# One scale chain in the quantised feed-forward, an fp32 value product in two attentions, and another routing order in mixer 3

## What is computed

```python
def _quantize_activations_groupwise(x):      # 5 groups along the batch
    ...
        gamma = jnp.max(jnp.abs(ag))
        xq = ... jnp.clip(ag * QB / (gamma + EPS), -QB + EPS, QB - EPS)
def _bitlinear(x, W, b):
    Wb = _binarize_weights_groupwise(W)
    y = jnp.einsum('btc,oc->bto', x, Wb) + b
    return _quantize_activations_groupwise(y)
h = _bitlinear(x, W1, b1)
h = jax.nn.gelu(h, approximate=False)
out = _bitlinear(h, W2, b2)

x = x + _L0_conv_ref(_ln_c(x), ...)   # then the feed-forward above, and so on
```

## Time and profile before

| | before |
|---|---|
| median of 3 runs | 862.85 us (858.54, 862.85, 864.74) |
| the profiled execution | 860.89 us |
| span of its trace | 859.1 us, so 1.8 us lie outside it |
| mean granted PE clock | 0.935 of full speed |
| busy share of the span | PE 91%, DVE 69%, POOL 65%, ACT 50% |

### The profile page before, as it was taken

How to read it: one execution, slowest core, us unless ns; L and a number is a source line. 1 busy time by engine, 2 the same in 40 slices (tenths; PEclk the granted TensorE clock), 3 DMA queues, 4 the chain that set the end, 5 groups by cost and what they waited for, 6 DMA issues and landing times.

```text
span 859.1 us, 27761 instructions
## 1 busy us (share of the span) xinstructions
PE 779.6 (91%) x10760; PEld 641.8 (75%) x10760; DVE 589.5 (69%) x1609; ACT 428.5 (50%) x777; POOL 556.4 (65%) x885
## 2 busy tenths in 40 slices
PE   4897678699899999969997999999799999999996
PEld 3776566588688888958876688888777776888886
DVE  6677477678577777848874477787776773776754
ACT  3564563366544444457773553535445555444441
POOL 5645523455287887867773687788565674788764
PEclk9696698799999999989998999999967999999999
DMA  6611100000311101000011011010000011110030
GB/s 165 125 12 30 35 1 2 2 3 3 78 54 36 50 28 29 3 1 2 0 46 30 28 31 30 27 56 3 2 1 2 0 29 29 33 55 27 28 84 20
DMA packets 39145, 26.17 MB, mean 30 GB/s; under 512 B 27132, under 2 KB 31981, under 8 KB 39045
## 3 DMA queue, kind: packets, MB, share of 16 engines
q1 hardware_dynamic: 38302, 24.41, 11.2%
q10 hardware_dynamic: 742, 0.38, 0.2%
HBM read 7.87 MB, written 1.57 MB: 11 GB/s over the span
## 4 chain that ended last, share of the span: by engine, by line
PE 81%; DVE 10%; ACT 3%; issue 3%; POOL 2%; POOLq 0%; ACTq 0%; DVEq 0%
PE PS L1679 22%; PE PS L1652 9%; PE PS L1653 8%; PE PS L1656 4%; PE PS L1401 3%; PE PS L1767 3%; PE PS L1754 3%; PE PS L1387 3%; PE PS L1778 2%; PE PS L1787 2%; PE PS L1388 2%; PE PS L1797 2%; PE PS L1568 2%; PE PS L1480 2%; PE PS L1847 1%
## 5 line engine op out<-in xcount | busy, mean ns | idle before, releaser
L712 ACT ACTIVATE H<-PS,B 128x512 f32<-128x512 f32 x288 | 173.7, 690 | 194.7 <-PE PS L1656 194.7
L1679 PEld LDWEIGHTS PS<-M,H 128*64 128x64 f32 x4608 | 192.3, 137 | 21.7 <-issue 17.5
L1679 PE MATMUL PS<-M,H 128*64 128x96 f32 x4608 | 205.1, 248 | 1.8 <-DVE X L1196 1.8
L1196 DVE SCALAR_TENSOR_TENSOR X<-PS,G,X 128x96 f32<-128x96 f32 (+1 forms) x384 | 121.7, 318 | 96.6 <-PE PS L1679 86.3
L480 POOL TENSOR_TENSOR msum<-stats 128x4 f32<-128x4 f32 (+1 forms) x61 | 16.1, 263 | 137.7 <-DVE stats L895 111.3
L1652 PE MATMUL PS<-XH,M1h 128*128 128x512 f32 x192 | 78.7, 410 | 0.0
L490 POOL TENSOR_TENSOR XN<-X,mean 128x384 f32<-128x384 f32 x56 | 47.0, 840 | 48.9 <-PE PS L1401 48.9
L1653 PE MATMUL PS<-FHL,M1l 128*128 128x512 f32 x192 | 77.3, 402 | 0.0
L516 POOL TENSOR_TENSOR PF<-G,B 128x1536 f32<-128x1536 f32 x24 | 66.2, 2759 | 10.2 <-DVE G L1187 10.2
L524 POOL TENSOR_TENSOR ex<-euler,dl 128x16 f32<-128x16 f32 x24 | 69.9, 2912 | 1.7 <-DVE dl L1160 1.6
L494 POOL TENSOR_TENSOR rs<-ve,half 128x4 f32<-128x4 f32 (+1 forms) x61 | 65.4, 1072 | 4.8
(11 more groups left out here) (245 smaller groups left out, 1818.3 us busy)
## 6 DMA issues: line engine op xcount, KB each, us to landing
FHL<-XH SPq DMA_DIRECT2D x36, 192.0 KB, 2.5
FHL<-XL SPq DMA_DIRECT2D x36, 64.0 KB, 2.1
X<-XH SPq DMA_DIRECT2D x12, 192.0 KB, 2.5
raw<-L_ffn_w SPq DMA_DIRECT2D x3, 576.0 KB, 5.1
M<-L_ffn_w SPq DMA_DIRECT2D x3, 576.0 KB, 5.0
XH<-XL SPq DMA_DIRECT2D x24, 64.0 KB, 1.9
out<-X SPq DMA_DIRECT2D x8, 192.0 KB, 2.6
X<-x SPq DMA_DIRECT2D x3, 384.0 KB, 6.7
```

What stands on the lines that cost most here:

```text
L712: act.activation(H[p][:, c, :], bank(UB[c]), ACT.Gelu, bias=B1[e][:, c:c + 1]).then_inc(gelu_a, 1)
L1196: ins = dve.scalar_tensor_tensor(xt(g, t), bank(4 + t % 2)[:, e * C:(e + 1) * C], G[:, t, e:e + 1], xt(g, t), ALU.mult, ALU.add)
L1679: ins = pe.matmul(Y[rows, x * C:(x + 1) * C], H[p][:, j, t * P + rows.start:t * P + rows.stop], M2[e][:, j, :], start=c == 0, stop=c == CH ...
```

## The change

It has three parts.

1. **Feed-forward.** The two chains of scales become one (`maxima`, `scale_rows`, `spread`, `scales`): the transpose takes two columns, the first maximum of group q and the second of group q-2. The product with `gdg` spreads both numbers. `Y2` has two buffers. The bias products of `down` are gone; POOL adds the bias to the copied result (`ffn_bias`), and for the last group DVE adds it on the way out of PSUM. On ACT `ffn_out(q-1)` stands behind the GELU of group q (before: ahead of it). `ffn_stats(2)` stands ahead of the last `X` sum of attention 0. The second absolute maxima of the last two groups share their stretch with the softmax of group 8, the first of attention 1, whose scores are now made ahead of the last `down` products.
2. **Attentions.** ACT makes a whole copy `XV` of each transposed group (`whole`), and V is one fp32 product by 8 pieces (`values`) in the place of 12 products in three terms. Its weights `WV` are fetched by three more transfers; two more rows of ones are set at the start. In attention 0 the products of k and q of group g+2 stand ahead of P times V of group g, and so do their copies on ACT.
3. **Mixer 3.** On ACT `routing_relu` stands ahead of the first `mix_image`; on DVE `routing_out` and `routing_star` stand ahead of `mix_x`.

The core of the diff:

```diff
+        def chain(q):
+
+            return sum(2 + 2 * (2 <= x < FG) for x in range(q))
+
...
-            for q in range(FG):
+            def ffn_rows(q):
                 normalise(q, EPS_T, FT, fst_v, fag_p, X[:, q * FT * C:(q + 1) * FT * C], FX, ft_pe, fxn_p)
+
+            def ffn_bias(r):
+                pool.wait_ge(y2_a, r + 1)
+                pool.tensor_tensor(Y2[r % 2], Y2[r % 2], b2bc[:].unsqueeze(1).to_broadcast([P, FT, C]), ALU.add).then_inc(y2_p, 1)
+
+            for q in range(4):
+                ffn_rows(q)
+            ffn_bias(0)
+            ffn_rows(4)
+            ffn_bias(1)
             prep(2, 1, 0)
+            ffn_bias(2)
+            ffn_bias(3)
             prep(2, 1, 1)
...
+            def whole(m, p):
+                after(act, xt_used, m - 1)
+                act.activation(XV[p][0:C, :], turned(m), ACT.Copy).then_inc(xv_a, 1)
...
+                    def copy_keys():
+                        after(act, s_pe, n + 2)
+                        if ka == 1:
+                            act.wait_ge(q_pe, n + 3)
+                            act.activation(qT[0:C, :], bank(QB01[1], 512, C), ACT.Copy, scale=QSCALE).then_inc(q_a, 1)
+                        act.wait_ge(k_pe, n + 3)
+                        if ka == 1:
+                            act.activation(KT[0:C, :], bank(KB[1], 512, C), ACT.Copy).then_inc(k_a, 1)
+                        else:
+                            for h in range(HEADS):
+                                rows = slice(h * DH, (h + 1) * DH)
+                                ins = act.activation(kT[rows, h, :], PS[rows, KB[0], :], ACT.Copy)
+                            ins.then_inc(k_a, 1)
+                            act.wait_ge(q_pe, n + 3)
+                            act.activation(qT[0:C, :], bank(QB01[0], 512, C), ACT.Copy, scale=QSCALE).then_inc(q_a, 1)
+
+                    if ka == 0 and has(g, 2):
+                        copy_keys()
...
                 if q == FG - 1:
                     prep_hi(8, 0)
-                if q > 0:
+                    whole(8, 0)
                     ffn_out(q - 1)
                 for c in range(CH):
                     act.wait_ge(cl_v, 3 * q + c + 1)
                     after(act, fd_pe, 2 * (q - 1))
                     act.activation(YH[q % 2][:, c, :], Y1[q % 2][:, c, :], ACT.Gelu, scale=qs[:, 0:1]).then_inc(ge_a, 1)
+                if 0 < q < FG - 1:
+                    ffn_out(q - 1)
...
-                if has(g, 1):
-                    mix_image(g, p, 0)
                 if has(g, 2, 2):
                     routing_relu(g + 2)
                 if has(g, 1):
+                    mix_image(g, p, 0)
                     mix_image(g, p, 1)
...
+            def scale_rows(q):
+                n = columns(q).stop - columns(q).start
+                dve.wait_ge(g_pe, 2 * q + 1)
+                dve.tensor_reduce(gmx[0:n], PS[0:n, 7, 0:P], AX.X, ALU.max).then_inc(gm_v, 1)
+                if n == 2:
+                    dve.wait_ge(gm_v, chain(q) + 3)
+                    dve.tensor_scalar(gdg[:], ident[0:2, 0:2], gmx[:], None, ALU.mult).then_inc(gm_v, 1)
+
...
+            for q in range(FG):
+                if q > 0:
+                    for c in range(CH):
+                        first_max(q, c)
+                if q >= 2:
+                    second_max(q - 2)
+                dve.wait_ge(ab_v, 3 * (q + 1))
+                dve.tensor_reduce(am1[:, 0:1], am[:, 0, 0:CH], AX.X, ALU.max).then_inc(gm_v, 1)
+                if q == 0:
+                    dve.wait_ge(fu_pe, 6)
+                    ffn_lo(1)
+                if q + 3 < FG:
+                    ffn_stats(q + 3)
+                if q >= FG - 2:
+                    dve.wait_ge(fxn_p, FG)
+                    prep_stats(8 + q - (FG - 2), q - (FG - 2), (xu[1], q - (FG - 2) + 1), None)
+                scale_rows(q)
+                if 0 < q and q + 2 < FG:
+                    dve.wait_ge(fu_pe, 6 * (q + 2))
+                    ffn_lo(q + 2)
+                if q == FG - 1:
+                    prep_lo(8, 0)
+                scales(q)
+                clip_first(q)
+                if q >= 2:
+                    add_second(q - 2)
+                if q == 0:
+                    dve.wait_ge(fu_pe, 12)
+                    ffn_lo(2)
...
+            second_max(FG - 2)
+            dve.wait_ge(s_pe, 9)
+            dve.tensor_reduce(top, scores(1), AX.X, ALU.max).then_inc(mx_v, 1)
+            scale_rows(FG)
+            dve.wait_ge(mx_v, 9)
+            dve.tensor_tensor(scu, scores(1), top.unsqueeze(3).to_broadcast([P, GT, HEADS, 64]), ALU.subtract).then_inc(sub_v, 1)
+            scales(FG)
+            add_second(FG - 2)
             prep_lo(9, 1)
...
+            ins.then_inc(y2_l, 1)
+            dve.wait_ge(y2_l, 1)
+            second_max(FG - 1)
+            dve.wait_ge(exp_a, 9)
+            dve.tensor_reduce(sm[:], scv, AX.X, ALU.add).then_inc(sum_v, 1)
+            scale_rows(FG + 1)
+            dve.wait_ge(sum_v, 9)
+            dve.reciprocal(rc[:], sm[:]).then_inc(rcp_v, 1)
+            dve.wait_ge(rcp_v, 9)
+            dve.tensor_tensor(PFC.rearrange("p (u j) -> p u j", j=64), scv, rc[:].unsqueeze(2).to_broadcast([P, HEADS * GT, 64]), ALU.mult)\
+               .then_inc(nrm_v, 1)
+            scales(FG + 1)
+            add_second(FG - 1)
+            prep_stats(10, 2, (xu[1], 2), None)
             attention(2, 1, (xu[1], FG))
...
-                if has(g, -1):
-                    mix_x(1, g - 1, xu[6])
                 if has(g, 1, 2):
                     routing_out(g + 1, 1 - p)
                 if has(g, 2, 2):
                     routing_star(g + 2)
+                if has(g, -1):
+                    mix_x(1, g - 1, xu[6])
...
+            def values(ka, x, k):
+                for t in range(GT):
+                    for rows in HALF:
+                        ins = pe.matmul(PS[rows, VW, t * C:(t + 1) * C], x[0:k, t * P + rows.start:t * P + rows.stop], WV[ka][0:k, :],
+                                        start=True, stop=True)
+                ins.then_inc(xt_used, 1)
...
+                    def keys_of():
+                        x = XH[p], XL[p]
+                        pe.wait_ge(lo_v, m + 3)
+                        if ka == 0:
+                            terms(bank(KB[0], 512, C), weights(1), x, k).then_inc(k_pe, 1)
+                        if more:
+                            pe.wait_ge(sub_v, n + 2)
+                        terms(bank(QB01[ka], 512, C), weights(0), x, k).then_inc(q_pe, 1)
+                        if ka == 1:
+                            pe.wait_ge(xv_a, m + 3)
+                            terms(bank(KB[1], 512, C), weights(1), x, k).then_inc(k_pe, 1)
+
+                    if ka == 0 and has(g, 2):
+                        keys_of()
                     if has(g, 0):
...
+            def maxima(q):
+
+                lo, hi = 0 if q < FG else 1, 2 if q >= 2 else 1
+                pe.wait_ge(gm_v, chain(q) + (hi - lo))
+                after(pe, qs_v, 2 * q - 1)
+                pe.transpose(PS[0:hi - lo, 7, 0:P], am1[:, lo:hi], ident[:]).then_inc(g_pe, 1)
+
+            def spread(q):
+                n = (2 if q >= 2 else 1) - (0 if q < FG else 1)
+                pe.wait_ge(gm_v, chain(q + 1))
+                pe.matmul(PS[:, 7, P:P + n], onesf[0:n, :], gdg[:] if n == 2 else gmx[0:1, :], start=True, stop=True).then_inc(g_pe, 1)
...
+                if q == 0:
+                    maxima(0)
                 if q == FG:
                     first_products()
-                for t in range(FT):
-                    if more:
-                        for j in ((0, 1, 2), (3,), (4,), (5,), (), ())[t]:
-                            ffn_up(q + 1, j)
-                    if t == 2 and r >= 0:
-                        second_max(r)
-                    if output and t < 3:
-                        down(q - 1, t)
-                    if t == 3:
-                        if r >= 0:
-                            second_scale(r)
-                        if q + 2 < FG:
-                            ffn_turn(q + 2)
-                        if q == FG - 1:
-                            pe.wait_ge(fl_v, FG)
-                            prep_turn(8, True)
-                        if q < FG:
-                            pe.wait_ge(gm1_v, 2 * q + 1)
-                            after(pe, qs2_v, 2 * r + 1)
-                            pe.transpose(PS[0:1, 7, 0:P], am1[:, 0:1], ident[:]).then_inc(g1_pe, 1)
-                    if t == 5 and q < FG:
-                        pe.wait_ge(gm1_v, 2 * q + 2)
-                        pe.matmul(PS[:, 7, P:P + 1], onesf[0:1, :], gmx[:, 0:1], start=True, stop=True).then_inc(g1_pe, 1)
-                    if output and t >= 3:
+                if more:
+                    for j in range(3):
+                        ffn_up(q + 1, j)
+                if q > 0:
+                    down(q - 1, 0)
+                if q + 2 < FG:
+                    ffn_turn(q + 2)
```

(72 more changed lines are left out.)

216 lines of the change are left out of this document (77 added, 139 removed).

## The result

The changed kernel takes 854.25 us (median of 14 runs, 847.8 to 857.2) against 863.39 us before (14 runs, 858.54 to 868.53). The ratio is 0.9887, 95% interval 0.986 to 0.9914: some 1.1% or 9 to 10 us faster. Some executions of the kernels here ran at a lower granted clock and over 1.5% above the fastest of the same kernel; the ratios leave these out, while the medians beside them do not. The forecast was 859.0 within 849 to 868, so the range held, but its sum of -3.1 us stands for what was nearly three times that. Its profiled execution has a span of 850.8 us against 859.1, which is 8.3 us less and agrees with the medians.

The account below looks back on a forecast made before the run. Bounds: PE in attention 1, the maximum-scale-clip chain in the feed-forward, mixer 3 in between, the engine ring in attention 0. Terms -0.6 + 3.5 - 3.0 - 3.0 = -3.1 us gave 859.0 us, range 849 to 868.

Parts of the forecast that it names:

- Mixer 3: Mixer 3: nearly all of PE's 3.5 us of waiting for hh goes; -3.0 us, bounds zero and -3.6.
- Feed-forward: Feed-forward: group 2 late, later groups faster, softmax lengthens the tail; about +3.5 us, range -6 to +8.
- The walk: Feed-forward: new order stepped through with old durations, giving clip 2 at 128.9 us, 5.3 us late.
- Attention 1: Attention 1: the cheaper value product shortens PE's chain by 0.43 us for each of 7 groups; -3.0 us.
- Attention 0: Attention 0: rows of ones cost +1.0 us, early value products give it back; about -0.6, between -2.5 and +1.
- R1: Feed-forward: the block in group 2 does not cost, clip 2 at 119.7 us; 850 us in all, chance 0.25.
- R2: Attentions: the fp32 value product is no cheaper than three terms; 863.5 us in all, chance 0.06.
- R3: Mixer 3: the next wait takes over the wait for hh; 862 us in all, chance 0.07.
- R4: Feed-forward: PE's low clock stays through groups 3 and 4; 869 us in all, chance 0.12.
- the likeliest case: Whole kernel: the forecast itself, 855.5 to 863 us by the bounds of the single terms; chance 0.50.

Follow-up runs that it names:

- m3_only: The kernel before with only the new routing order of mixer 3 on ACT and DVE: 857.55 us, 0.9912 of before.
- no_m3: The changed kernel with the new routing order of mixer 3 undone: 861.67 us, 0.9981 of before.
- dve_half: The kernel before with only DVE's new order in mixer 3, routing_out and routing_star ahead of mix_x: 862.77 us, 1.0006 of before.
- delay_star: The changed kernel with an unread maximum over 768 columns on DVE ahead of routing_star in mixer 3: 858.26 us, 0.9976 of before.
- rows_first: The changed kernel, but POOL normalises feed-forward group 4 before adding the bias of group 0: 848.22 us, 0.982 of before.
- stats_early: The changed kernel with the statistics of group 10 moved on DVE ahead of the softmax sum of group 8: 849.38 us, 0.9869 of before.
- late_ones: The changed kernel with XV's two rows of ones set behind the second group's statistics: 854.2 us, 0.9899 of before.
- all_three: The changed kernel with the edits of rows_first, stats_early and late_ones together: 844.41 us, 0.9789 of before.
- fill_wait: The kernel before with six unread products on PE ahead of its wait for hh in mixer 3: 868.41 us, 1.0058 of before.
- fill_short: The kernel before with three unread products on PE ahead of its wait for hh in mixer 3: 865.24 us, 1.0022 of before.

## Why the prediction came out as it did

**Mixer 3 is the step that was mis-sized.** It read: PE waits 3.5 us for `hh`, "nearly the whole wait goes in each body", -3.0 us, with bounds of zero and -3.6. The waits did go. But the stage gave 8.8 us in the trace and some 8 by the medians of m3_only, and of no_m3 against the changed kernel. The term counted the wait at its length and left out the clock. The row had a sign of it: the stage of the earlier trace rows ran at 0.86 with a PE that is busy nine tenths of the time. Each body paused PE for 0.7 us at the same place. Without the pauses the same 906 records take 7.4 us less. All the traces sort by this. Where PE waits for `hh` in each body (before, no_m3, dve_half, delay_star), the 906 records take 95.7 to 99.9 us and the stage 101.6 to 107.8. Where it doesn't (the changed kernel, m3_only, rows_first, stats_early, late_ones, all_three), they take 91.5 to 93.5 us and the stage 96.3 to 97.7. With filler in the wait they take 92.0 and 93.2. A low clock in the second to fourth tens of microseconds of the stage is in all of them, as 0.79, 0.50 and 0.85 before; it is what comes behind that differs. From 40 us into the window on, it stays at 1.00 in five of the six traces without the wait, and falls to 0.67 to 0.87 in two or more of the tens where the wait is. Why a pause of 0.7 us brings it down, no run here shows. The term's tacit claim that the halves on ACT and DVE each give a part was also wrong: only both together do anything.

**Feed-forward.** The walk held point by point. Clip of group 1: 110.9 forecast, 110.68 in the trace. Transposes of group 4 behind a PE pause of some 6 us: 5.71. Clip 2: 128.9 and 129.23. Clip 3: 137.7 and 137.77. Clip 4: 146.45 and 146.81. Statistics of group 10: 164.3 and 164.94. The doubled durations behind the pause were right (granted clock 0.57 between clips 1 and 2). The term was +3.5 and is +4.1. Clip 1 to clip 2 is 18.5 us in no_m3, delay_star, stats_early and late_ones too. That the walk named the cause is shown by rows_first, which removes it; that it named the way into attention 1 by stats_early. What the walk left out is PE's wait of 2.9 us for ACT's copy ahead of the first `down` tile; it did not show in the changed kernel, because POOL's wait ended later.

**Attention 1.** The value product takes 0.81 us on the chain, as taken from the row of its shape:

```profile
185.26 0.81 PE PS L1523 x16
...
191.95 0.23 PE PS L1523
```

The period between these two starts is 6.69 us, against 7.04. That is -0.35 a group where -0.43 was forecast, and -2.5 in all for -3.0.

**Attention 0.** -0.7 for -0.6, with +1.08 at the start as taken from the earlier trace rows. The closeness is in part luck of the execution: in no_m3, delay_star and stats_early, whose attention 0 is the same code, the second group of the feed-forward comes at 75.4 to 75.6 us and not at 77.52. There the granted clock from 30 to 35 us is 0.98 to 1.00, where it is 0.50 in the trace read above and in the one of before. So the term is -0.7 to -2.9 us, which the bound of -2.5 nearly covers.

**The rivals.** R1 (no block in group 2) did not happen. R2 fell: 16 records take 0.81 us. The estimate of 1.28 us from the four passes of the Trainium skill's page "FP8 and Floating Point Precision", section "TensorE Precision Notes", does not hold for these products, and the measurement decides. Whether they need fewer passes, or the two halves of 64 tokens overlap on the array, no run here shows. R3 (mixer 3 gives nothing) fell, and the truth lay on its other side, though of the 3.5 us of waiting some 2 did pass to other waits, as R3 feared. R4 asked for groups 3 and 4 at the low clock; they ran at 0.92 and 1.00, and not always so: in stats_early and late_ones clip 3 came 10.5 and 10.8 us behind clip 2, at a clock of 0.74 and 0.72.

Three of the four terms had the right sign and size, and the sum was off by the one that looked safest. That the range held is luck in part: 854.25 us lies under the 855.5 to 863 of the likeliest case, in the part of the range that was kept open for R1, and R1 did not happen.

## What to carry to other kernels

Price a short wait of PE that returns in each body by what the clock of the stage shows, not by its length: where PE is busy nine tenths of a stage and the granted clock is still under 0.9, such waits here cost a little over twice what they last (8 us for 3.5, 5.2 for 2.1). Look on an engine that isn't the bottleneck for what stands at the head of its queue waiting (POOL's bias sum) while its next work is ready and another engine needs it. And where a value depends on two engines' orders, change both before judging either.

## What was not expected of the hardware

The feed-forward differs from one execution to the next, though its code is the same. From the statistics of its second group to those of group 10 it takes 83.8 us in the trace of before, 83.5 in m3_only and in dve_half, but 89.8 in fill_wait and 90.0 in fill_short; the granted clock from 75 to 163 us is 0.79 in the first three and 0.71 in fill_short. Attention 0 of the changed kernel differs by 2 us in the same way. So where the low stretches fall, in a phase where PE pauses often, is not the same in each execution, and a single trace of such a phase is uncertain by some 6 us; effects under that were read here by medians, or by start times inside one execution. What decides between the two lengths is open.
